# Turning the next expert's rows on VectorE and by a DMA through DRAM, in place of TensorE transposes, in a mixer and mixture-of-experts kernel

## The reference

```python
scores = (tanh(xf @ gate_w.T) + 1.0) * 0.5           # 8 experts
vals, idx = top_k(scores.T, k)                       # each expert takes its 1024 best rows
y = layernorm(xf[idx], gamma, beta)                  # k x 512 for each expert
h = gelu(y @ fc1[n].T + b1[n])                       # 512 -> 2048
o = h @ fc2[n].T + b2[n]                             # 2048 -> 512
out = xf.at[idx].add(o * vals)
```

## Time and profile before

| | before |
|---|---|
| median of 3 runs | 2657.49 us (2655.19 to 2657.57) |
| profiled execution | 2657.18 us |
| its span, first to last instruction | 2655.4 us |
| TensorE busy | 2629.0 us (99%) |
| TensorE weight loads | 2136.6 us (80%) |
| VectorE busy | 2050.7 us (77%) |
| ScalarE busy | 1498.4 us (56%) |
| GpSimd busy | 676.9 us (25%) |
| DMA, share of 16 engines | q1 23.1%, q0 14.8% |

### The profile page before, as it was taken

The page is one execution under the profiler, slowest core; times in us unless marked ns, Lnnn a source line. Parts: engine busy times, 40 slices in busy tenths (PEclk is TensorE's granted clock), DMA queues, the critical chain, the costliest instruction groups (busy, mean ns, idle before and its releaser), DMA issues.

```text
span 2655.4 us, 39102 instructions
## 1 busy us (share of the span) xinstructions
PE 2629.0 (99%) x11816; PEld 2136.6 (80%) x11816; DVE 2050.7 (77%) x3514; ACT 1498.4 (56%) x2578; POOL 676.9 (25%) x1006
## 2 busy tenths in 40 slices
PE   8999999999999999999999999999999999999998
PEld 4588888888888888888888888888888888888886
DVE  8778888888888888788876768867788677786654
ACT  5744555555555565565545555665555655556553
POOL 5422222221222222223432214113141131321102
PEclk9999999999999999999999999999999999999999
DMA  9733222223333322235443425234253342533413
GB/s 365 261 127 111 80 94 87 90 93 111 111 112 111 111 73 83 92 95 161 151 133 110 116 67 145 80 96 131 64 142 85 93 132 67 136 91 88 100 56 72
DMA packets 139664, 300.28 MB, mean 113 GB/s; under 512 B 26224, under 2 KB 26352, under 8 KB 135664
## 3 DMA queue, kind: packets, MB, share of 16 engines
q1 hardware_dynamic: 105840, 201.54, 23.1%
q0 software_dynamic: 33664, 96.75, 14.8%
HBM read 244.46 MB, written 53.77 MB: 112 GB/s over the span
## 4 chain that ended last, share of the span: by engine, by line
PE 95%; DVE 1%; DMA 1%; issue 1%; ACT 1%; POOL 0%; SPq 0%; POOLq 0%; DVEq 0%; ACTq 0%
PE po L2530 9%; PE po L2532 9%; PE po L2531 9%; PE ring L1584 9%; PE ring L1585 8%; PE ring L1586 8%; PE pb L2530 4%; PE pb L2531 4%; PE pb L2532 4%; PE po L1622 4%; PE po L1623 4%; PE po L1624 4%; PE pc L2530 2%; PE pc L2531 2%; PE pc L2532 2%; PE pb L571 1%
## 5 line engine op out<-in xcount | busy, mean ns | idle before, releaser
L2530 PE MATMUL po<-w2h,hid_h 128*128 128x512 f32 x1024 | 402.1, 393 | 0.1
L1584 PE MATMUL ring<-xt_h,w_h 128*128 128x512 f32 x1024 | 400.1, 391 | 0.1
L2531 PE MATMUL po<-w2l,hid_h 128*128 128x512 f32 x1024 | 398.6, 389 | 0.0
L1585 PE MATMUL ring<-xt_l,w_h 128*128 128x512 f32 x1024 | 398.5, 389 | 0.0
L1586 PE MATMUL ring<-xt_h,w_l 128*128 128x512 f32 x1024 | 398.4, 389 | 0.0
L1373 DVE SCALAR_TENSOR_TENSOR u<-xin,cw,u 128x512 f32<-128x512 f32 x384 | 288.5, 751 | 75.8 <-issue 47.0
L2013 POOL DMA_INDIRECT out_dram<-res,idx_c x64 | 108.7, 1699 | 477.0 <-DVE res L2377 465.9
L1584 PEld LDWEIGHTS ring<-xt_h,w_h 128*128 128x128 f32 x1024 | 192.2, 188 | 40.9 <-DVE xt_l L542 0.9
L1586 PEld LDWEIGHTS ring<-xt_h,w_l 128*128 128x128 f32 x1024 | 192.2, 188 | 40.2
L2530 PEld LDWEIGHTS po<-w2h,hid_h 128*128 128x128 f32 x1024 | 192.3, 188 | 39.5 <-DVE hid_l L2367 0.5
L1585 PEld LDWEIGHTS ring<-xt_l,w_h 128*128 128x128 f32 x1024 | 192.3, 188 | 39.4
(11 more groups left out here) (300 smaller groups left out, 6307.5 us busy)
## 6 DMA issues: line engine op xcount, KB each, us to landing
w2r<-fc_in SPq DMA_DIRECT2D x256, 256.0 KB
wo<-wo_halves POOLq DMA_DIRECT2D x120, 512.0 KB, 4.5
w1r<-fc_in SPq DMA_DIRECT2D x144, 256.0 KB
x_tail<-x_in SPq DMA_DIRECT2D x64, 256.0 KB, 2.7
out_dram<-res SPq DMA_DIRECT2D x64, 256.0 KB, 2.0
g_x<-x_in SPq DMA_DIRECT2D x15, 1024.0 KB, 8.3
xt_rows<-g_xnt SPq DMA_DIRECT2D x15, 1024.0 KB, 9.9
rows<-xt_rows SPq DMA_DIRECT2D x15, 1024.0 KB, 6.2
```

The source lines that it names most:

```text
L1584: pe.matmul(ring[r % 2][:, :], w_h[:, r, q], xt_h[:, k, :], start=(k == 0), stop=False)
L1585: pe.matmul(ring[r % 2][:, :], w_h[:, r, q], xt_l[:, k, :], start=False, stop=False)
L2530: pe.matmul(dst, ah, bh, start=start, stop=False, skip_group_check=more)
L2531: pe.matmul(dst, ah, bl, start=False, stop=False, skip_group_check=more)
```

## The change

The 32 transposes of each Strassen expert go from TensorE. The rows `rows[0]` and `rows[1]` are, after their normalisation, turned in place by VectorE in blocks of 32 x 32 (`row_turn`, eight instructions an expert: two in each of pairs 2 to 5). SyncE then stores them to a DRAM buffer `turned` so that the blocks come to their places (`rows_out`: four DMAs a tile, whose shortest runs are 32 floats): `b_out(0)` in its step q = 5, `b_out(1)` in q = 6. When both stores have landed, VectorE makes the four sums in place, in the rows themselves (`t_sum`, eight instructions, in pair 7 around ADD_LOW); `t_out` stores these too (8 DMAs). The operands are loaded back whole (`b_back`: six DMAs of 256 KB; `t_back`: eight), and ScalarE and VectorE make the high and low halves as before, in another order of slots. GpSimd's gather of the rows after these waits for the landing of `t_out`.

```diff
+        def rows_out(i, kind, sem):
+            d = turned[2 * kind + i].rearrange("(t c) (j q p) -> q c j t p", c=QUAD, q=P // QUAD, p=QUAD)
+            for q in range(P // QUAD):
+                sp.dma_start(d[q], rows[i][q * QUAD:(q + 1) * QUAD, :, :].rearrange("c j (t p) -> c j t p", p=QUAD)
+                             ).then_inc(sem, 16)
+        def b_out(e, i):
+            sp.wait_ge(c_t, turned_at(e, i, J - 1) + 1)
+            rows_out(i, 0, c_b_out)
+        def t_out(e):
+            sp.wait_ge(c_tr, sum_at(e, "T4", 1) + 1)
+            for i in range(2):
+                rows_out(i, 1, c_t_out)
+        def parts_back(e, free, *names):
+            sp.wait_ge(c_p1, free + 1)
+            for name in names:
+                for k in range(2):
+                    sp.dma_start(tw[name][k], source(name)[k * P:(k + 1) * P, :]
+                                 ).then_inc(back(e, name)[0], 16)
+        def b_back(e, free):
+            sp.wait_ge(c_b_out, XT_STORED + 128 * e)
+            parts_back(e, free, "B11", "B21", "B22")
+        def t_back(e, free):
+            sp.wait_ge(c_t_out, XT_STORED + 128 * e)
+            parts_back(e, free, "T2", "T1", "T3", "T4")
...
# sync, expert 0
+            if n == FT + 7:
+                b_out(1, 0)
+                b_out(1, 1)
+            if n == FT + 8:
+                b_back(1, FT)
+            if n == FT + 10:
+                t_out(1)
+            if n == FT + 11:
+                t_back(1, FT)
# sync, expert(e), after the loads of pair q
+                if q == 5 and not last:
+                    b_out(e + 1, 0)
+                if q == 6 and not last:
+                    b_out(e + 1, 1)
# sync, expert(e), after load_2 of tile x
+                if x == FT and not last:
+                    t_out(e + 1)
+                    b_back(e + 1, products(e, PAIRS - 1, P3))
+                if x == FT + 1 and not last:
+                    t_back(e + 1, products(e, PAIRS - 1, P3))
# gpsimd
-                pool.wait_ge(c_t, bank_at(e, 1, "B21") + 1)
+                pool.wait_ge(c_t_out, XT_STORED + 128 * e)
# scalar, t_high
-            if name[0] == "B":
-                bank = R3 if name == "B21" else R1
-                act.wait_ge(c_t, bank_at(e, k, name) + 1)
-                act.copy(tw[name][k], bank[:, :]).then_inc(c_th, 1)
-                act.copy(th[name][k], bank[:, :]).then_inc(c_th, 1)
-            else:
-                act.wait_ge(c_tr, sum_at(e, k, name) + 1)
-                act.copy(th[name][k], tw[name][k]).then_inc(c_th, 1)
+            act.wait_ge(*back(e, name))
+            act.copy(th[name][k], tw[name][k]).then_inc(c_th, 1)
# vector
+        def row_turn(e, i, j):
+            dve.wait_ge(c_nm, J * (2 * e + i) + j + 1 + 1)
+            dve.transpose(rows[i][:, j, :], rows[i][:, j, :]).then_inc(c_t, 1)
+        def t_sum(e, name):
+            a, b = SUM_OF[name]
+            dve.wait_ge(c_t, turned_at(e, 1, J - 1) + 1)
+            dve.wait_ge(c_b_out, XT_STORED + 128 * e)
+            for h in range(2):
+                here = slice(2 * h, 2 * h + 2)
+                if name != "T1":
+                    dve.wait_ge(c_tr, sum_at(e, SUMS[SUMS.index(name) - 1], h) + 1)
+                dve.tensor_tensor(part(name)[:, here, :], part(a)[:, here, :], part(b)[:, here, :],
+                                  ALU.subtract).then_inc(c_tr, 1)
# vector, pair q: after ADD_FIRST
+            elif not last:
+                t_sum(e + 1, "T1")
+                t_sum(e + 1, "T3")
# vector, pair q: after ADD_LOW
+            elif not last:
+                t_sum(e + 1, "T2")
+                t_sum(e + 1, "T4")
+            if 2 <= q <= 5 and not last:
+                for j in (2 * (q % 2), 2 * (q % 2) + 1):
+                    row_turn(e + 1, (q - 2) // 2, j)
# tensor, expert(e)
-            if not last:
-                t_bank(e + 1, 0, "B11")
-                t_bank(e + 1, 0, "B12")
...
-                for k, name in () if last else T_BANK_AT.get(x, ()):
-                    t_bank(e + 1, k, name)
+T_HIGH_AT = {2: ("B11",), 3: ("B21",), 4: ("T2",), 5: ("T1",), 7: ("T3",), 8: ("T4",), 9: ("B22",)}
+T_LOW_AT = {3: ("B11",), 4: ("B21",), 5: ("T2",), 6: ("T1",), 8: ("T3",), 9: ("T4",), 10: ("B22",)}
+FIRST_SUM_AT = {6: ("T1", "T3"), 7: ("T2", "T4")}
+FIRST_HIGH_AT = {8: ("B11",), 9: ("B21",), 12: ("T2", "T1"), 13: ("T3", "T4"), 14: ("B22",)}
+FIRST_LOW_AT = {9: ("B11",), 10: ("B21",), 13: ("T2", "T1"), 14: ("T3", "T4"), 15: ("B22",)}
```

More of the change, by code:

```diff
@@ L1829, in stage_experts @@
     rows = [ew.rows, ew.rows1]
+    turned = t["turned"]
     yt_h = [xt_h, ew.w1[:, 4:8, :]]
@@ L1846, in stage_experts @@
     c_tr = m.count("f_tr")
+    c_b_out, c_t_out = sums.c_xt_store[0], sums.c_xt_store[1]
+    c_back = [sums.c_xt_store[2]] + ends.c_xt[0:4]
+    XT_STORED, X_LOADED = 16 * NB // 4 + 1, 16 * NB + 1
     c_wh = m.count("f_wh")
@@ L1888, in shared_ahead, with turned_at, sum_at, part @@
         return 128 * e - 128 + (shared(0, 28 + x) if x < 4 else shared(0, 24 + x))
-    def bank_at(e, k, name):
-        return 8 * e + 4 * k + BANKS.index(name) + 1
+    def turned_at(e, i, j):
+        return 8 * e + 4 * i + j + 1
+    def sum_at(e, name, h):
+        return 8 * e - 8 + 2 * SUMS.index(name) + h + 1
     def high_at(e, k, name):
-        return 20 * e - 12 + 10 * k + HIGHS.index(name) + 1
+        return 14 * e - 6 + 2 * PARTS.index(name) + k + 1
     def low_at(e, k, name):
-        return 14 * e - 6 + 7 * k + LOWS.index(name) + 1
-    def sum_at(e, k, name):
-        return 8 * e - 8 + 4 * k + SUMS.index(name) + 1
+        return 14 * e - 6 + 2 * PARTS.index(name) + k + 1
+    def part(name):
+        i, half = PLACE[name]
+        return rows[i][:, :, half * HALF:(half + 1) * HALF]
+    def source(name):
+        i, half = PLACE[name]
+        return turned[i + (2 if name[0] == "T" else 0)][half * HALF:(half + 1) * HALF, :]
+    def back(e, name):
+        x = PARTS.index(name)
+        if x == 0:
+            return c_back[0], XT_STORED + 32 * e
+        if name in LATE_BACK:
+            return c_back[4], X_LOADED + 96 * e
+        return c_back[x], X_LOADED + 32 * e
     def gathered(e, i):
@@ L2223, in second_half @@
             for x in range(FT):
-                for k, name in () if last or x == 0 else T_HIGH_AT.get(x, ()):
-                    t_high(e + 1, k, name, free)
+                for name in () if last else T_HIGH_AT.get(x, ()):
+                    for k in range(2):
+                        t_high(e + 1, k, name, free)
                 if FT + x + 2 < 2 * FT:
@@ L2259, in scalar @@
             if g == 1:
-                for k, name in FIRST_HIGH_AT.get(s, ()):
-                    t_high(1, k, name, FT)
+                for name in FIRST_HIGH_AT.get(s, ()):
+                    for k in range(2):
+                        t_high(1, k, name, FT)
                 if s == FT - 2:
@@ L2439, in second_half @@
             for x in range(FT):
-                for step in () if last or x == 0 else T_LOW_AT.get(x, ()):
-                    t_step(e + 1, step, free)
+                for name in () if last else T_LOW_AT.get(x, ()):
+                    for k in range(2):
+                        t_low(e + 1, k, name)
                 if FT + x + 2 < 2 * FT:
@@ L2501, in vector @@
                 row_low(T_AT.index(s - 1))
+            if g == 0 and s >= FT - 2:
+                for j in (2 * (s - FT + 2), 2 * (s - FT + 2) + 1):
+                    row_turn(1, 0, j)
             if g == 1:
-                for step in FIRST_LOW_AT.get(s, ()):
-                    t_step(1, step, FT)
+                if 1 <= s <= J:
+                    row_turn(1, 1, s - 1)
+                for name in FIRST_SUM_AT.get(s, ()):
+                    t_sum(1, name)
+                for name in FIRST_LOW_AT.get(s, ()):
+                    for k in range(2):
+                        t_low(1, k, name)
                 if s == FT - 2:
@@ L2543, in trn @@
             turned(pt[k % 2], 1, k)
[L2545 to L2560, removed]
         def hidden(g, s):
@@ L2695, in stage_experts @@
     return sync, gpsimd, vector, tensor, scalar
[L2698 to L2720, removed]
-                10: ((1, "sum", "T3"), (1, "sum", "T2"), (1, "low", "T1")),
-                11: ((1, "low", "B22"), (1, "low", "T3")),
-                12: ((1, "sum", "T4"), (1, "low", "B21")),
-                13: ((1, "low", "T2"), (1, "low", "T4"))}
+T_HIGH_AT = {2: ("B11",), 3: ("B21",), 4: ("T2",), 5: ("T1",), 7: ("T3",), 8: ("T4",), 9: ("B22",)}
```

40 lines of the change are left out of this document (6 added, 34 removed).

## The result

The changed kernel takes 2754.6 us in the median (2752.86 to 2757.25), the kernel before 2656.7 us in the same session: a ratio of 1.037, 95% interval 1.0352 to 1.0388. It is 98 us slower. Forecast were 2707 us and slower, with a range from 2640 to 2795: the sign and the range held, the size was half of what came.

The account below looks back on a forecast made before the run. TensorE, busy 99% of the span, was taken as the bound. Per expert -3.7 + 4.2 + 7.2 + 0.3 = +8.0 us, six times 48, plus 2 for the first, took 2657.2 to 2707 us; range 2640 to 2795.

Parts of the forecast that it names:

- What transposes cost: On TensorE, the 32 transposes removed per expert give back 3.7 us, 26 us over seven preparations.
- The piece's price: In the turned-row stores, each 128 B piece takes 11 ns per DMA engine, bounds 9.4 and 16.
- Wait 1: Last pair: VectorE waits for tile 1's store before its sums; TensorE gaps of 2.6 and 1.6, together 4.2 us an expert.
- 1.6 us for hid_low(15): After the last product, hid_low(15) comes late behind ADD_LOW: TensorE gap of 1.6 us, even if the tile lands early.
- rival A: Faster: the store's tile lands before VectorE's idle time and B11 in time, so the waits are covered; 2641 us, 17%.
- Wait 2: Before tile 20, ScalarE waits for B11, queued behind t_out: TensorE gap of 7.2 us an expert, from 2.0 to 15.9.
- earlier gather: The next rows' gather starts some 17 us earlier, moving 2 MB beside t_back and eating margin; not priced.
- first preparation: Expert 1: stores land late for the sums and hid_low(23); gap 5.6 us against 3.7 saved, net +2.
- The turns: Eight more VectorE instructions an expert in pairs 2 to 5, 0.60 us each: gap of 0.3 us (0 to 3.6).
- B: Much slower: pieces cost several times the estimate because neighbours lie 64 KB apart in DRAM; 2850 us, 12%.
- C: A draw: the last-pair wait comes as forecast, but tile 20 is in time; 2662 us, 6%.

Follow-up runs that it names:

- kernel with all changes: Changed kernel with turns and b_out earlier, t_out and b_back in step q = 7, T4 behind ADD_LOW, new slots, earlier first-preparation stores: 2635.8 us.
- filled kernel: Changed kernel with idle TensorE matmuls added in experts 1 to 6, 11 before the wait on ADD_LOW and 42 inside tile 19's share: 2748.8 us.
- kernel with both edits: Changed kernel with stores in runs of 2 KB (wrong operands) and without the first group's scatter in experts 1 to 6: 2663.4 us.

## Why the prediction was right and where it was off

*What transposes cost: nearly right.* 3.7 us an expert was all that an expert takes beyond 720 matmuls at 0.2267 us. Without the stores it takes 163.63 us, so 3.3 were the transposes', and 0.4 stay without them.

*The piece's price: right.* 11 ns was the estimate, 9.4 and 16 the bounds. With the stores alone on the engines, in the kernel with all changes, the view of 1588 to 1597 us has

```profile
DMA packets 12673, 1.63 MB, mean 181 GB/s; under 512 B 12672, under 2 KB 12672, under 8 KB 12672
```

that is 11.4 ns a piece and engine. Without the scatter, 12,666 packets of the queue take 11 us (1609 to 1620), 13.9 ns.

*Wait 1: right, but for its second half.* Landing 8.7 us after the issue was worked out, 9.0 came. Gap 2.6 worked out, 2.85 in this expert, 3.3 in the mean. The 1.6 us for hid_low(15) behind it is there where ADD_LOW is late and the matmuls are not slow (1.28 in the filled kernel and 1.3 with runs of 2 KB), but the changed kernel hides it behind slow matmuls: 0.6 us in one expert and none in five. Together 3.4 us, where the sum had 4.2. That the 1.6 us stay even if the tile lands early is wrong: the kernel without the stores and the one with the stores a pair earlier have no gap there. hid_low(15) itself waits 2.08 us for ScalarE in the trace of before, and in the latter kernel it still waits 1.06; the sums fit into VectorE's idle time, which that sentence, and with it rival A's sum, left out.

*Wait 2: right in its place and chain, mis-sized.* The sum gave 3.7 us if the scatter doesn't disturb and 10.8 if engines are simply shared, and I took the middle, 7.2. Measured are 10.9, and 5.2 without the scatter. The choice of the middle is the step that was wrong: the row said that the scatter's queue alone kept the engines 86.7% busy, and the stores of pieces fill them too (in the changed kernel, for b_out's tile, 95.6% from 1591 to 1595 us); the two then add up. That the simple sum, 10.8, is so near to 10.9 is in part luck: the share without the scatter was 1.5 us too small and the scatter's, 5.7 where 7.1 was said, 1.4 too large. This term is 22 of the 48 us by which I was short. The earlier gather, which wasn't priced, made no gap behind tile 20.

*Slow matmuls: a term that the sum doesn't have, and the largest part of the miss.* The trace of before has no gap in TensorE here, so it has no slow matmul either, but its beginning has one of 2.7 us that ends at 18.74, and I didn't read what came behind it (bounds and us, TensorE, clock, DMA share, GB/s):

```profile
20.00:21.00 1.00, 1.00 (x7) 0.50 1.07 414
```

By the rows of the changed kernel it is 1.8 + 2.7 us an expert, 27 of the 48. Taking them away would not give all of it back: what lies before tile 20 is made up by a longer gap there, as the filled kernel showed.

Together, an expert of the changed kernel is 182.3 us (the first b_out issue on the chain at 1587.22 and, five experts later, at 2498.77), 15.4 more than 166.96. The terms as measured: -3.3 + 3.3 + 0.1 + 10.9 + 1.8 + 2.7 = 15.5 (the slow matmuls from one expert, the gaps in the mean), where the prediction had 8.0. Six of them are 92 us. The first preparation had a gap of 6.7 us (5.6 said), with its slow matmuls, and two gaps of 1 us at the start of expert 1; it brings the rest, about 5 net where 2 was said.

*The turns: as said.* 0.69 us each (the line of the transpose: 56 of them, 687 ns), no gap in pairs 2 to 5; the 0.3 us wasn't needed.

*The rivals.* A falls: the tile lands 9.0 us after its issue, not in 6.1. B falls twice: the pieces cost 11 to 14 ns, and moving them next to one another changes nothing. The Trainium skill (VectorE: DVE Perf Modes, The three transpose paths) gives its factor of 19 against the crossbar for a plain DMA whose innermost destination stride is large. No run here has such a DMA or the crossbar, so nothing here bears the factor out or refutes it. What the runs show is that, with blocks already turned, t_out in runs of 128 B takes twice the issue time of runs of 2 KB (19.2 against 9.7 us). C falls with wait 2.

## What to carry to other kernels

When a transfer is to take work off a full engine, don't ask what it costs but when its reader wants it and what else is on the DMA engines in that time: here the same stores cost 98 us as the change had them, and the kernel was 21 us faster than the one before with t_out issued 12 us earlier within the expert (counted from the loads of w1 ahead of it), before the scatter, b_out a pair or two earlier, and the readers in later slots. Where two loads on a shared resource are each near full, add them; the middle between adding and ignoring is no estimate. Price what comes behind a gap too: the slow matmuls were 4.5 us an expert. And look at what is queued in order behind a wait: a stand of ScalarE for a late load was a gap of TensorE in slot 2 and nothing in slot 3.

## What the runs showed of the hardware

TensorE can fall to the lower of its two clocks behind short gaps. In the changed kernel (bounds and us, TensorE busy, clock, DMA share, GB/s), behind the gap of 2.85 us, late in the gap of 12.7 us, and behind it; last, in the filled kernel, behind a gap of 3.01 us:

```profile
1600.50:1603.50 3.00, 3.00 (x8) 0.50 0.00 0
1624.50:1632.00 7.50, 0.00 (x0) 0.50 1.01 269
1632.50:1637.50 5.00, 5.00 (x12) 0.50 1.05 411
...
1813.85:1818.00 4.15, 4.15 (x18) 1.00 1.03 390
```

TensorE is busy all through the first and the third stretch and granted half of its clock, 1.2 GHz: 12 matmuls in 5 us, where the last stretch has 18 in 4.15. In the first the DMA engines are idle, so it isn't they that slow the matmuls. Gaps of 2.85 and 2.46 us have ten slow matmuls behind them, one of 3.01 us has none, and gaps of up to 2.0 us, in the kernel with both edits, leave the mean clock at 0.998. So the length of the gap alone doesn't tell, and what else decides these runs don't show.

A store of 2048 pieces of 128 B holds SyncE itself. Its issue (ns: shortest, median, longest):

```profile
L1951 SPq DMA_DIRECT2D turned<-rows x112: 583/1573/4191, 1416.9 to 2534.1; - x112
```

That is 1.6 us in the median and up to 4.2, where a load of 256 KB back takes 0.43. All that SyncE has to issue next waits for that, the weights too: behind the three loads of w2 that end at 1605.10 the next one is issued at 1628.60.
